# Conv2 in 21 matmuls a chunk instead of 24, with the work around it put in another order

## The chip, the cores and the metric

One core of a Trainium2 chip runs one launch that handles all 8 images. The metric is the time of that launch on the device in microseconds, lower is better. PE is the matmul engine, DVE, ACT and POOL are the vector, scalar and GpSimd engines, SP is the engine that here only issues DMAs. Each works through its own list of instructions, and semaphores tie the lists together.

## The reference, cut to what matters

x has shape 8 x 64 x 64 x 48. Four layers follow each other:

```python
# L0: linear attention over the 4096 pixels, then three convolutions, 96 channels inside
y = concatenate([attention(x), x])                # 96 channels
y = leaky_relu(conv1x1(y, w1) + b1, 0.2)          # conv1
y = leaky_relu(conv3x3(y, w2) + b2, 0.2)          # conv2, SAME padding, 96 -> 96
x1 = conv1x1(y, w3) + b3 + x                      # w3, 96 -> 48
# L1: relu, depthwise 3x3, pointwise 48 -> 48, batch norm
x2 = bn(pointwise(depthwise(relu(x1))))
# L2: experts mixed for each image
rw = sigmoid(mean(x2) @ Wr + br)                  # routing, 4 experts
h = relu(bn(x2 @ mix(Wpw, rw)))                   # expand, 48 -> 192
h = relu(bn(depthwise3x3(h, mix(Wdw, rw))))       # depthwise, 192 channels
x3 = bn(h @ mix(Wpwl, rw)) + x2                   # project, 192 -> 48
# L3: like L1
out = bn(pointwise(depthwise(relu(x3))))
```

## The kernel before

An image is cut into 8 chunks of 8 rows (512 pixels) at 96 channels, or 4 chunks of paired rows (`pair_conv`, m = 0 to 3) at 48 channels. Pairs means that two halves of the image lie beside each other on the partitions (even from row 0, odd from row 64).

The images are pipelined in three parts. In iteration f, PE runs conv2, w3, L1 and the first two expand chunks of image f; the attention and conv1 of image f+1 (`attn`); and the project, L3 and output of image f-1 (`back`), whose depthwise DVE computes beside conv2. The first iteration stands alone (no `back`), a hardware loop runs f = 1 to 6, and `last_iteration` finishes images 6 and 7 alone. The order on each engine is written out by hand in `iteration` of that engine; nothing else schedules.

What the steps below touch:

- **conv2** (L1247, L1252, L1258). The fp32 product is made of reduced-precision parts: high activations by low weights (9 taps, `w2_l` x `y1_h`, 96 rows), high activations and the last third of the low ones by high weights (9 taps, 128 rows, `w2_h` x part 0 of `y1_parts`), and the other two thirds of the low activations by high weights, packed over 128 rows (6 matmuls, `w2_two`, `w2_one`). `copy_thirds` on SP places the thirds after POOL (L1116) has computed the low part.
- **L1 and L3** (`l1`, `l3` = `pair_conv`, L1285 to L1288): 15 matmuls a chunk. Each chunk needs six DMAs (`copy_beside`, `beside_l1`, `beside_l3`) that place shifted copies beside the activations. They wait for the high and low parts of chunk m+1 as well (ACT, then DVE L789).
- **Depthwise** (L696): 48 steps of one tap over 1024 elements on DVE, and two first taps, in an order set by `tap_of_step`; how many stand beside each chunk of conv2 and between the later steps is the table `steps_at`. `project(back, (m,))` (L1334 to L1350) waits for the units that it reads, made nonnegative by ACT (`finish_unit`, L1549).
- **x2** is L1's output, high and low, in `y1_parts`. `copy_x2` moves it to `x_even` and `x_odd`, from which expand and project read, in 8 DMAs on SP (L1007).
- **Routing** (DVE L807, L809, PE L1294, DVE L814, ACT L1607): the mean over L1's output decides the mixed weights (`mix_weights`). The halo (`expand_halo`, first matmuls of L1300 and L1301) is the first to read them and x2.
- **Attention**: `transpose_x` (L1170), scores (L1181), squares on ACT, `norms_begin` on DVE (L619 to L621), `scale_k` on POOL (L1110), sums (L1193), gather, weights.

## Time and profile before

| | |
|---|---|
| Time, median of 3 runs | 1107.56 us (1106.48 to 1109.27) |
| The profiled execution, its own time | 1108.68 us, of which the span from first to last instruction is 1106.9 us |
| PE | 1030.5 us busy, 93% of the span |
| DVE | 872.8 us busy, 79% |
| ACT, POOL | 469.6 us and 92.6 us busy |
| Granted TensorE clock | 0.975 of full speed on average |
| DMA | one hardware queue, 86.84 MB |

Six iterations of the loop lie between 176.28 and 927.8 us of the span. The stretch ahead of them is the prologue and the first iteration, the one behind them the last. Lines such as L1285 are lines of the kernel before; a number in brackets at the end of a row is idle time just before it and what ended it.

### The profile page before, as it was taken

Reading aid. Unit: us, or ns where it says so; the run is one execution under the profiler, and the core shown is the slowest. Engines: PE = TensorE matmul, PEld = TensorE weight load, DVE = VectorE, ACT = ScalarE, POOL = GpSimd, SP = SyncE. Lnnn points to the kernel's source line nnn. Section 1 sums busy time; section 2 is a strip of 40 time slices with the busy share of each in tenths; the row PEclk is TensorE's granted clock in tenths of the full one; section 3 lists DMA queues with packets and bytes.
Section 4 is the critical chain, followed back from the end, with each engine's and each line's share of the span. In section 5 each row is a group of like instructions: output and inputs, shape, how many; then the busy total and the mean of one; then the engine's idle time right before and its main releaser. Section 6 shows DMA issues by size and latency. Waiting matters only on the chain.

```text
span 1106.9 us, 14973 instructions
## 1 busy us (share of the span) xinstructions
PE 1030.5 (93%) x4790; PEld 658.3 (59%) x4790; DVE 872.8 (79%) x1201; ACT 469.6 (42%) x813; POOL 92.6 (8%) x72
## 2 busy tenths in 40 slices
PE   4689969999999999999999999999999999999976
PEld 3456656666665676666665576666666576655524
DVE  6652579997699958998599958998599958998950
ACT  3311434345633645345632645255532645234431
POOL 0300012001300102001300103001300103000000
PEclk9799969999999999999999999999999999998998
DMA  5125416145432556145342456145442453146214
GB/s 70 41 57 76 99 30 102 26 98 122 91 51 50 107 125 101 24 97 114 85 62 49 103 127 105 24 89 110 96 64 49 103 116 74 22 86 137 40 26 101
DMA packets 124401, 87.19 MB, mean 79 GB/s; under 512 B 96880, under 2 KB 97749, under 8 KB 124373
## 3 DMA queue, kind: packets, MB, share of 16 engines
q1 hardware_dynamic: 124372, 86.84, 39.9%
q8 instruction: 15, 0.25, 0.1%
q14 instruction: 14, 0.11, 0.0%
HBM read 10.82 MB, written 6.29 MB: 15 GB/s over the span
## 4 chain that ended last, share of the span: by engine, by line
PE 70%; DVE 12%; issue 7%; SPq 4%; ACT 3%; DMA 3%; POOL 0%; ACTq 0%; DVEq 0%; POOLq 0%
PE bank L1247 13%; PE bank L1252 12%; PE bank L1258 8%; PE bank L1285 8%; PE bank L1228 5%; PE bank L1300 3%; PE bank L1269 3%; PE bank L1301 3%; DMA y_parts<-a_parts 2%; DVE s L619 2%; DVE a_parts L789 2%; PE bank L1350 2%; PE bank L1288 2%; DVE dwa L696 2%; PE bank L1287 2%
## 5 line engine op out<-in xcount | busy, mean ns | idle before, releaser
L696 DVE SCALAR_TENSOR_TENSOR dwa<-h1a,dyn,dwa 128x1024 f32<-128x1024 f32 x224 | 274.1, 1275 | 0.0
L1247 PE MATMUL bank<-y_parts,w_l 96*96 96x512 f32 x576 | 151.4, 408 | 0.0
L1252 PE MATMUL bank<-y_parts,w_h 128*96 128x512 f32 x576 | 147.3, 400 | 0.0
L696 DVE SCALAR_TENSOR_TENSOR dwb<-h1b,dyn,dwb 128x1024 f32<-128x1024 f32 x112 | 136.6, 1275 | 0.0
L1285 PE MATMUL bank<-a_parts,wt_h 128*112 128x512 f32 x384 | 118.1, 416 | 15.1 <-DMA y_parts<-a_parts 10.9
L1247 PEld LDWEIGHTS bank<-y_parts,w_l 96*96 96x96 f32 x576 | 91.6, 163 | 60.7 <-issue 21.3
L1252 PEld LDWEIGHTS bank<-y_parts,w_h 128*96 128x96 f32 x576 | 93.3, 162 | 44.2
L1285 PEld LDWEIGHTS bank<-a_parts,wt_h 128*112 128x112 f32 x384 | 64.0, 177 | 49.1 <-issue 23.1
L1116 POOL TENSOR_TENSOR y_parts<-y,y_parts 96x512 fp32r<-96x512 f32 x56 | 67.1, 1200 | 248.0 <-DVE y L750 248.0
L1561 ACT ACTIVATE y<-bank,b2s 96x512 f32<-96x512 f32 x32 | 21.9, 684 | 141.0 <-PE bank L1258 141.0
L1258 PE MATMUL bank<-y_parts,w_one 128*96 128x512 f32 x192 | 77.1, 401 | 0.0
L1258 PE MATMUL bank<-y_parts,w_two 128*96 128x512 f32 x192 | 76.7, 399 | 0.0
L1110 POOL TENSOR_TENSOR tok<-tok,u 128x1536 f32<-128x1536 f32 x8 | 24.6, 3073 | 586.3 <-DVE u L621 586.3
L1228 PE MATMUL bank<-xq,w_cur 97*96 97x512 f32 x128 | 68.1, 614 | 3.6 <-DVE y L750 3.6
L789 DVE SCALAR_TENSOR_TENSOR a_parts<-v,a_parts 112x512 fp32r<-112x512 f32 x64 | 59.0, 932 | 15.7 <-ACT a_parts L1590 12.9
L1561 ACT ACTIVATE xq<-bank,b2s 96x512 f32<-96x512 f32 x32 | 21.9, 685 | 116.0 <-PE bank L1258 107.4
L749 DVE TENSOR_TENSOR y_parts<-bank,y 96x512 fp32r<-96x512 f32 x64 | 43.9, 687 | 24.9 <-ACT y L1517 24.8
L1612 ACT ACTIVATE dwa<-bank,conv_bias,inv 112x512 f32<-112x512 f32 x28 | 21.8, 778 | 91.2 <-PE bank L1288 91.2
L1285 PE MATMUL bank<-a_parts,wt_l 128*112 128x512 f32 x192 | 56.6, 403 | 0.0
L1288 PE MATMUL bank<-y_parts,wt_h 128*112 128x512 f32 x128 | 51.3, 401 | 0.0
L1287 PE MATMUL bank<-y_parts,wt_h 128*112 128x512 f32 x128 | 51.1, 399 | 0.0
L1181 PE MATMUL bank<-qkw,xcm 113*128 113x192 f32 x256 | 49.4, 337 | 1.7 <-ACT xcm L1477 1.7
(263 smaller groups left out, 1714.3 us busy)
## 6 DMA issues: line engine op xcount, KB each, us to landing
y_parts<-a_parts SPq DMA_DIRECT2D x64, 198.0 KB, 3.0
y_parts<-a_parts SPq DMA_DIRECT2D x64, 197.6 KB, 3.4
tok<-in_x_dram SPq DMA_DIRECT2D x48, 192.0 KB, 4.9
a_parts<-a_parts SPq DMA_DIRECT2D x128, 66.0 KB, 2.4
y_parts<-y_parts SPq DMA_DIRECT2D x64, 131.9 KB, 2.3
x_even<-y_parts SPq DMA_DIRECT2D x32, 198.0 KB, 3.6
x_odd<-y_parts SPq DMA_DIRECT2D x32, 198.0 KB, 4.0
out_dram<-dwb SPq DMA_DIRECT2D x24, 192.0 KB, 3.6
```

The lines of the kernel that those rows point to most:

```text
L696: nc.vector.scalar_tensor_tensor(out=dst, in0=tap_input(n, t), scalar=weight, in1=dst, op0=ALU.mult, op1=ALU.add).then_inc(tap_step, 1)
L749: nc.vector.tensor_tensor(y1_view(y1_h, k - 1), bank.rearrange("p (j w) -> p j w", w=W), y1_tokens(k - 1), ALU.max).then_inc(y1h_ready, 1)
L789: return nc.vector.scalar_tensor_tensor(out=lo[:, rows, 1:W + 1], in0=src[:, m % 2, :].rearrange("p (j w) -> p j w", w=W), scalar=0.0, in1 ...
L1116: nc.gpsimd.tensor_tensor(y1_view(y1_l, k), y1_tokens(k), y1_view(y1_h, k).bitcast(F32), ALU.subtract).then_inc(y1l_ready, 1)
L1181: last = nc.tensor.matmul(bank[:, m * 2 * C2:(m + 1) * 2 * C2], xcm[:, i * 128:(i + 1) * 128], qkw[:, :], start=True, stop=True)
L1228: nc.tensor.matmul(bank[0:C2, :], w1_cur[:, :], xq[:, (k - 1) % 2, :], start=True, stop=True)\
L1247: nc.tensor.matmul(bank[0:C2, :], w2_l[:, t, :], y1_h[:, rows, cols], start=t == 0, stop=False)
L1252: nc.tensor.matmul(bank[0:C2, :], w2_h[:, t, :], y1_parts[:, 0, rows, cols], start=False, stop=False)
L1258: last = nc.tensor.matmul(bank[0:C2, :], wgt[:, kh, :], y1_parts[:, 1, rows, cols], start=False, stop=kh == 2 and kw == 2)
L1285: nc.tensor.matmul(bank[0:P2, :], wgt[layer][:, kw, :], own[:, rows, kw:kw + W], start=n + kw == 0, stop=False)
L1287: nc.tensor.matmul(bank[0:P2, :], wgt[layer][:, 3, :], beside[:, rows, 1:W + 1], start=False, stop=False)
L1288: last = nc.tensor.matmul(bank[0:P2, :], wgt[layer][:, 4, :], beside[:, rows, 2:W + 2], start=False, stop=n == 2)
```

## The change

- Conv2 takes 9 + 9 + 3 matmuls a chunk. `w2_l` grows to 128 rows (its last 32 hold high weights of the middle third), so that `y1_parts` part 0 carries the high activations and the low middle third. Part 1 is a copy of the high activations with the last low third. The first low third lies three times, shifted by 0, 1 and 2 columns, in `y1_low`, a tile of its own. This tile shares its memory with the attention's `tok`.
- So `copy_thirds` issues 5 DMAs a piece instead of 3 (one of 96 x 1056 values), POOL clears the edges of `y1_low` for each image, and `load_x` (next image's x into `tok`) waits for the end of conv2. It stands between `beside_l1` for quarters 0, 1 and for quarters 2, 3. DVE rewrites the column of ones in `tok` each iteration.
- The depthwise units run in the order of the projections: (0,2), (1,3), (4,5), with `steps_at` 6,3,3,4,3,4,3,3 beside conv2 and 3,1,4,13 behind it.
- PE: l1(1) stands ahead of project 0 and 1, all of `transpose_x` behind l1(2), l3(0) ahead of project 2 (in bank 1), all 32 sums ahead of the routing.
- `copy_x2` is 4 DMAs of twice the size, issued by ACT behind the routing's sigmoid instead of by SP in two halves. In the last iteration it stays on SP.
- The last iteration: l3(0) of image 6 ahead of the routing, l3(1) to l3(3) between expand chunks, the taps on PE in two parts, and units 3 and 4 of the last depthwise one behind the other instead of by turns.

```diff
-B_COPIES, WT_COPIES, X2_COPIES = 6, 24, 8
+B_COPIES, WT_COPIES, X2_COPIES = 6, 24, 4
...
+        with nc.sbuf_tensor("y1_low", [128, (H + 2) * WP], F32R) as y1_low:
+            y1_l = y1_low[0:C2, :].rearrange("p (h w) -> p h w", w=WP)
+        tok = sb("tok", [128, RUN, 2, TOK])
...
+        STEPS = in_turn(0, 2) + in_turn(1, 3) + in_turn(4, 5)
+        FINISHED = {0: 2, 1: 4, 2: 5, 3: 6}
-        steps_at = (0,) * CHUNKS + (7, 4, 4, 4, 4, 4, 4, 4) + (1, 1, 5, 8)
+        steps_at = (0,) * CHUNKS + (6, 3, 3, 4, 3, 4, 3, 3) + (3, 1, 4, 13)
...
-        LAST_STEPS = ([(n, t) for t in range(TAPS) for n in (0, 1)] + [(n, t) for t in range(1, TAPS) for n in (3, 4)]
-                      + [(5, t) for t in range(1, TAPS)])
+        LAST_STEPS = in_turn(0, 1) + in_turn(3) + in_turn(4) + in_turn(5)
...
             def iteration(f, attn, back):
                 conv2_out(f, back)
+                if attn is not None:
+                    nc.vector.memset(tok[:, :, :, ONE_AT], 1.0)
...
+                norms_begin(attn)
                 x2_low_part(f, 0)
+                if back is not None:
+                    l3_low_part(back, 2)
                 x2_low_part(f, 1)
-                norms_begin(attn)
                 x2_low_part(f, 2)
                 if back is not None:
-                    l3_low_part(back, 2)
+                    l3_low_part(back, 3)
                 mean_out(f)
                 x2_low_part(f, 3)
                 route(f)
-                if back is not None:
-                    l3_low_part(back, 3)
...
         def load_x(sp, image):
-            wait(sp, xqt_done, CHUNKS * image)
+            wait(sp, conv2_done, CHUNKS * image)
...
+                wait(sp, y1h_ready, CHUNKS * image + 2 * p + 2)
+                sp.dma_start(second[0:C2, :], first[0:C2, :]).then_inc(apart_copied[p], 16)
                 wait(sp, y1l_ready, POOL_CHUNKS * image + min(2 * p + 2, POOL_CHUNKS))
...
+                sp.dma_start(first[C2:128, :], low[THIRD:2 * THIRD, :]).then_inc(apart_copied[p], 16)
+                sp.dma_start(second[C2:128, :], low[2 * THIRD:C2, :]).then_inc(apart_copied[p], 16)
+                wait(sp, apart_copied[p], 48 * (image + 1))
+                for shift in (1, 2):
+                    sp.dma_start(low[shift * THIRD:(shift + 1) * THIRD, :-shift], low[0:THIRD, shift:]).then_inc(shifts_copied[p], 16)
...
                 route(f)
-                if attn is not None:
-                    fourth_powers(attn)
-                if back is not None:
-                    l3_out(back, (0,))
+                act.wait_ge(x2l_ready, PCHUNKS * f + PCHUNKS)
+                copy_x2(act)
+                fourth_powers(attn)
```

PE, conv2, one chunk in the loop. Before:

```order
L1247 MATMUL bank<-y_parts,w_l 96x512 x9
L1249 ISA
L1252 MATMUL bank<-y_parts,w_h 96x512 x9
L1254 REGISTER_ALU
L1258 MATMUL bank<-y_parts,w_two 96x512
L1258 MATMUL bank<-y_parts,w_one 96x512
L1258 MATMUL bank<-y_parts,w_two 96x512
L1258 MATMUL bank<-y_parts,w_one 96x512
L1258 MATMUL bank<-y_parts,w_two 96x512
L1258 MATMUL bank<-y_parts,w_one 96x512
```

The change:

```order
L1249 REGISTER_ALU
L1253 MATMUL bank<-y_parts,w_l 96x512 x9
L1253 MATMUL bank<-y_parts,w_h 96x512 x9
L1256 REGISTER_ALU
L1259 MATMUL bank<-y_low,w_row 96x512 x3
L87 REGISTER_ALU
```

The six single matmuls of `w_two` and `w_one` are gone; three of `w_row` stand in their place.

PE, from project 3 (`pick`, `pc`) to the first sums (`tok`) and the chunk of L3 (`wt_h`) that follows. Before, with the routing (`routed`) ahead of l3(0) and then the first half of the sums:

```order
L1334 MATMUL bank<-x_odd,pick 112x512
L1335 MATMUL bank<-x_even,pick 48x512
L1350 MATMUL bank<-dwa,pc 48x512 x2
L1350 MATMUL bank<-dwb,pc 48x512 x2
L1294 MATMUL bank<-wr,routed 128x4
...
L1285 MATMUL bank<-a_parts,wt_h 112x512 x3
L1287 MATMUL bank<-y_parts,wt_h 112x512
L1288 MATMUL bank<-y_parts,wt_h 112x512
...
L1193 MATMUL bank<-tok 48x97 x16
```

The change, where the chunk of L3 behind the routing is l3(1):

```order
L1331 MATMUL bank<-x_odd,pick 112x512
L1332 MATMUL bank<-x_even,pick 48x512
L1347 MATMUL bank<-dwa,pc 48x512 x2
L1347 MATMUL bank<-dwb,pc 48x512 x2
...
L1196 MATMUL bank<-tok 48x97 x32
L1290 MATMUL bank<-wr,routed 128x4
...
L1281 MATMUL bank<-a_parts,wt_h 112x512 x3
L1283 MATMUL bank<-y_parts,wt_h 112x512
L1284 MATMUL bank<-y_parts,wt_h 112x512
```

All 32 sums moved ahead of the routing, and l3(0) ahead of both projections; between the routing and l3(1) PE has nothing.

SP, between L3's first quarter and the next. Before, the first half of x2 is copied there:

```order
L945 REGISTER_ALU
L1007 DMA x_even<-y_parts 48x1056 x2
L1007 DMA x_odd<-y_parts 48x1056 x2
...
L972 DMA a_parts<-a_parts 16x2x528 x2
L972 DMA y_parts<-a_parts 16x2x528
L972 DMA y_parts<-a_parts 48x2x528
L976 DMA y_parts<-a_parts 16x2x527
L976 DMA y_parts<-a_parts 48x2x527
```

SP in the change, at the place where the loads of x stand, ahead of L1's quarter 2 (`a_parts`, then `y_parts`):

```order
L947 ISA
L960 ISA
L960 DMA tok<-in_x_dram 64x16x48
L960 ISA
L960 DMA tok<-in_x_dram 64x16x48 x3
L960 ISA
L960 DMA tok<-in_x_dram 64x16x48
L960 ISA
L960 DMA tok<-in_x_dram 64x16x48
L947 REGISTER_ALU x2
L974 DMA a_parts<-a_parts 16x2x528 x2
L974 DMA y_parts<-a_parts 16x2x528
```

The x2 copies left SP altogether, and the six loads of x moved from its start to this place, past two quarters of L1.

## Rows read from the trace of the kernel before

**Rows 1.** The page, section 1: busy microseconds, share of the span, instructions.

```profile
span 1106.9 us, 14973 instructions
...
PE 1030.5 (93%) x4790; PEld 658.3 (59%) x4790; DVE 872.8 (79%) x1201; ACT 469.6 (42%) x813; POOL 92.6 (8%) x72
```

**Rows 2.** Windows, one iteration of the loop: length, then busy time of each engine.

```profile
426.60:551.95 125.35, 122.34 (x589) 78.70 (x589) 106.85 (x137) 58.15 (x100) 11.51 (x8) 1.00 0.43 85
```

**Rows 3.** Windows, conv2 and the middle of one loop iteration.

```profile
426.60:475.99 49.39, 49.39 (x205) 31.59 (x206) 49.35 (x49) 13.95 (x17) 0.00 (x0) 1.00 0.34 53
475.99:515.90 39.91, 38.79 (x202) 23.82 (x200) 35.89 (x44) 25.55 (x50) 3.12 (x1) 1.00 0.49 102
```

**Rows 4.** Timeline of PE, the last part of one chunk of conv2 and the next.

```profile
436.60 0.40 PE L1258 MATMUL bank<-y_parts,w_two 128*96 128x512 f32 x1
...
438.02 2.30 PE L1247 MATMUL bank<-y_parts,w_l 96*96 96x512 f32 x9
```

**Rows 5.** Timeline of PE, from the end of project 2 to the halo.

```profile
502.45 1.03 PE L1350 MATMUL bank<-dwb,pc 128*48 128x512 f32 x4
...
510.21 0.35 PE L1294 MATMUL bank<-wr,routed 112*128 112x4 f32 x2 [0.66 <-DVE routed L809]
510.43 0.96 PE L1285 MATMUL bank<-a_parts,wt_h 128*112 128x512 f32 x3
...
514.16 1.54 PE L1193 MATMUL bank<-tok 128*48 128x97 f32 x32
516.69 0.94 PE L1285 MATMUL bank<-a_parts,wt_h 128*112 128x512 f32 x3 [0.98 <-DMA y_parts<-a_parts]
...
531.38 0.28 PE L1300 MATMUL bank<-x_even,ew_h 96*128 96x64 f32 x1
```

**Rows 6.** Timeline of DVE and POOL in the same stretch.

```profile
489.08 1.29 DVE L789 SCALAR_TENSOR_TENSOR a_parts<-v,a_parts 112x512 fp32r<-112x512 f32 x2
...
490.29 9.65 DVE L696 SCALAR_TENSOR_TENSOR dwa<-h1a,dyn,dwa 128x1024 f32<-128x1024 f32 x8
...
501.76 3.35 DVE L619 TENSOR_REDUCE s<-tok 128x64 f32<-128x3072 f32 x1 [0.61 <-ACT tok L1487]
...
506.01 3.12 POOL L1110 TENSOR_TENSOR tok<-tok,u 128x1536 f32<-128x1536 f32 x1 [79.50 <-DVE u L621]
...
506.39 3.29 DVE L789 SCALAR_TENSOR_TENSOR a_parts<-v,a_parts 112x512 fp32r<-112x512 f32 x1
```

**Rows 7.** Timeline of SP: DMA issues of x, L3's first copies, x2's second half.

```profile
431.36 5.79 SPq L958 DMA_DIRECT2D tok<-in_x_dram  x6
...
509.77 1.32 SPq L972 DMA_DIRECT2D a_parts<-a_parts  x2
...
522.96 1.22 SPq L1007 DMA_DIRECT2D x_even<-y_parts  x2
```

**Rows 8.** Timeline of DVE and PE, end of the first iteration.

```profile
133.49 3.35 DVE L619 TENSOR_REDUCE s<-tok 128x64 f32<-128x3072 f32 x1 [4.60 <-ACT tok L1487]
...
141.08 0.56 PE L1294 MATMUL bank<-wr,routed 112*128 112x4 f32 x2 [4.62 <-DVE routed L809]
...
141.57 5.01 PE L1193 MATMUL bank<-tok 128*48 128x97 f32 x64
...
153.74 0.42 PE L1300 MATMUL bank<-x_even,ew_h 96*128 96x64 f32 x1
```

**Rows 9.** Timeline of PE, end of the last iteration.

```profile
1040.33 23.36 PE L1328 MATMUL bank<-h1a,tok 128*128 128x512 f32 x54
...
1068.35 0.49 PE L1334 MATMUL bank<-x_odd,pick 96*112 96x512 f32 x1 [2.33 <-ACT dwa L1538]
...
1080.03 0.94 PE L1285 MATMUL bank<-a_parts,wt_h 128*112 128x512 f32 x3 [4.07 <-DMA y_parts<-a_parts]
```

**Rows 10.** Windows behind two idle times of PE: the third value from the end is the granted clock.

```profile
141.57:146.35 4.78, 4.78 (x65) 4.78 (x64) 3.95 (x15) 2.89 (x3) 0.00 (x0) 0.53 0.64 150
1068.35:1075.00 6.65, 6.65 (x28) 1.88 (x30) 3.52 (x6) 3.94 (x6) 0.00 (x0) 1.00 0.06 10
```

More of the change, by code:

```diff
@@ L186, in conv_chain_kernel @@
         y1_parts = sb("y1_parts", [128, 2, H + 2, WP], F32R)
-        y1_h, y1_l = (y1_parts[0:C2, part, :, :] for part in range(2))
+        y1_h, y1_h_again = (y1_parts[0:C2, part, :, :] for part in range(2))
         y2 = [t[0:C2, 0:2, :].rearrange("p a n -> p (a n)") for t in (xq, y1)]
@@ L318, in tap_input, with step_value @@
             return src[:, r0 + t // 3:r0 + t // 3 + UNIT_ROWS, t % 3:t % 3 + W]
[L320 to L333 removed]
+        def step_value(image, n, t):
+            return TAP_STEPS * image + STEPS.index((n, t)) + 1
         def last_unit(n):
@@ L982, in copy_thirds @@
                 rows = slice(1 + p * H // PIECES, 1 + (p + 1) * H // PIECES)
-                high, low = (y1_parts[:, part, rows, :].bitcast(F32).rearrange("p h w -> p (h w)") for part in range(2))
+                first, second = (y1_parts[:, part, rows, :].bitcast(F32).rearrange("p h w -> p (h w)") for part in range(2))
+                low = y1_l[:, rows, :].bitcast(F32).rearrange("p h w -> p (h w)")
+                wait(sp, y1h_ready, CHUNKS * image + 2 * p + 2)
+                sp.dma_start(second[0:C2, :], first[0:C2, :]).then_inc(apart_copied[p], 16)
                 wait(sp, y1l_ready, POOL_CHUNKS * image + min(2 * p + 2, POOL_CHUNKS))
@@ L1016, in store, with beside_l1 @@
                     sp.dma_start(dst[j, par][:, runs, :], src[:, par, runs, :]).then_inc(stored, 16)
-        def beside_l1(sp, f):
-            for m in range(PCHUNKS):
+        def beside_l1(sp, f, quarters):
+            for m in quarters:
                 chunks = min(m + 2, PCHUNKS)
@@ L1274, in pair_conv @@
                 for m in chunks:
-                    if layer == L3 and image is LAST - 1 and m == 0:
-                        pe.wait_ge(ah3_ready, PCHUNKS * image + 1)
-                        bank = ring.bank(places[m])
-                    else:
-                        bank = ring.take(pe, image, places[m])
+                    bank = ring.take(pe, image, places[m]) if places[m] is not None else first_l3
                     pe.wait_ge(b_copied[layer][m], 16 * B_COPIES * (image + 1))
@@ L1638, in iteration @@
                 l1_high_part(f, PCHUNKS - 1)
[L1639 to L1640 removed]
+                if back is not None:
+                    finish_unit(back, 1)
+                    finish_unit(back, 3)
                 l1_out(f, (0,))
```

298 lines of the change are left out of this document (138 added, 160 removed).

## The prediction

> **What bounds the kernel now.** I first read the page's busy times: PE works 1030.5 of 1106.9 us [rows 1]. Such a share says that matmuls taken away should show, unless something else stands close behind. Then the windows: an iteration of the loop takes 125.35 us with PE busy for 122.34 and DVE for 106.85, and the clock is full [rows 2]. By stage, DVE is as busy as PE beside conv2 (49.35 of 49.39 us) and has 35.89 of the next 39.91 [rows 3]. So the loop has two limits. PE sets the pace of conv2, but from its end on a second chain runs nearly abreast: depthwise on DVE, project on PE, the low part on DVE, six DMAs, then L3. Its places are in the timelines: the last eight depthwise steps begin at 490.29 and take 9.65 [rows 6], project 2 ends at about 503.4, the first copies behind it are issued at 509.77 [rows 7], and the chunk of L3 that needs them starts at 516.69, having waited 0.98 for a DMA [rows 5]. The question is how much of what PE saves reaches the halo, which starts at 531.38 [rows 5]; conv1 and expand behind it are not touched.
>
> **Conv2's matmuls.** Six of them take 438.02 - 436.60 = 1.42 us [rows 4], 0.237 each. Three fewer in 8 chunks are 5.7 us an image, 45.6 us over 8 images. The whole of conv2 would end at 470.3 instead of 475.99 in this iteration. POOL's six small memsets and SP's two more DMAs a piece lie in the 20 us of conv1, where I cost them at nothing: conv2 of the next image reads the pieces one by one, and the cover is the 6 us that one chunk of conv2 lasts (an eighth of 49.39, rows 3). If it is gone, they cost up to 1 us an image.
>
> **From conv2 to L3 in the loop.** A chunk of L1 or L3 takes 3.73 us in the trace (510.43 to the sums at 514.16 [rows 5]); inside a dense stretch I take 3.65. Project takes 2.4 a chunk, w3 and each 8 transposes 1.0, four groups of scores 3.0, half of the sums 1.5 (1.54 for the 32 matmuls, rows 5). From 470.3: l1(0), w3, l1(1) and two projections end at 483.4. Next is l1(2). Its copies now stand on SP behind the six loads of x, and these wait for the end of conv2. They take 5.79 us to issue [rows 7], so until about 477.9. From a quarter's first issue to its matmul it is 516.69 - 509.77 = 6.92 us [rows 5, 7]. So l1(2) can start at 484.8, a **new wait of 1.4 us** (up to 1.9, since the loads of x still move when the copies start). Before, x was loaded at 431.36 [rows 7], beside conv2, and delayed nobody. Then come l1(2), all transposes with 0.5 us until ACT has handed the last over, the scores with l1(3) between, and 0.7 for the squares: 501.5. L3's chunk 0 goes to 505.2 and project 2 to 507.6. That is **4.2 us later than project 2 ends now**, although conv2 is 5.7 shorter, because l3(0), l1(3) and half of the scores are ahead of it. DVE's depthwise ends at about 501 instead of 499.94 [rows 6]: its steps are the same work and it has waits of 2 to 3 us for PE and ACT. It would bound project 2 only if PE were some 4 us faster.
>
> **What DVE and POOL do there.** Norms come ahead of the low parts now. The low part of L3 at 506.39 took 3.29 us [rows 6] where two others take 1.29 together (at 489.08, rows 6), and POOL's scaling runs over the same time (3.12 from 506.01 [rows 6]). In the change this clash meets the low part of x2 instead (norms 501.1 to 505.2), and L3's low part of chunk 2, which waits for project 2 anyway, is ready at 507.6 + 1.3 (ACT) + 0.7 = 509.6. So the clash leaves the chain, and this gives back what the later project 2 costs: SP issues at 509.6, now it does at 509.77. L3's chunk 1 starts at 516.5, now 516.69. The Trainium skill, "SBUF — State Buffer", on the shared port pair, says that a DVE operation with two SBUF inputs and a GpSimd operation that reads SBUF hold this pair as an exclusive lock and the loser blocks; these two rows agree.
>
> **The gap.** PE has project 3 until 510.0, sums until 513.0, routing at 513.2, then nothing before 516.5: **an idle time of 3.3 us**, where before l3(0) and sums stood. What PE saved in conv2 lies idle here and in the waits above (3.3 + 1.4 + 0.5 + 0.7 = 5.9). Behind it the quarters' copies follow at SP's pace of some 4.4 us (six issues of about 0.66, two in 1.32 in rows 7, and waits), so l3(2) starts at about 521.0 and l3(3) at 525.4, and the halo at 525.4 + 3.7 + weights and output tokens 1.3 = 530.4. Now it is 531.38. The gain is **1.0 us an iteration**, from 0.7 to 1.2 by the rounding of these steps, 6 us in six.
>
> **x2 on ACT's queue.** SP loses eight DMAs of about 0.6 us of issuing, the last four from 522.96 [rows 7]; none is on the chain, since L3's copies go first. On ACT the four stand behind the sigmoid, about 515.5 to 518, and hold back the fourth powers by 2.6 us, which gather then has to absorb. They move 1.6 MB beside L3's quarters 2 and 3. In the trace all goes over one queue, so it shows no two side by side. Bounds: nothing (the bytes fit into the gaps between quarters), or all of their time, which is 4 x 198 KB in the 3.25 us of issuing and landing twice over, 7 us. I take nothing for the likeliest case and come back to the rest below.
>
> **The first iteration loses.** It has no projections and no L3 as cover. The copies for l1(2) wait behind the x loads (about 5.4 us of PE idle, against 5.7 saved in conv2), and the last scores come later: squares end at 137, now at 133.49 [rows 8]. Norms, POOL's scaling and now all sums are ahead of the routing. Routing is at 141.08 [rows 8]. In the change the sums start at 144.3 (137.1 + 4.1 + 3.1) and take 2.95 at full or 5.01 as they do now [rows 8] at the lower clock, so routing is at 147.4 to 149.8. The 12.7 us from it to the halo (153.74, rows 8) are DVE's and ACT's and stay. Cost: +6.3 to +8.7, taken as **+7.5**.
>
> **The last iteration gains.** Conv2 gives 5.7, and the chunks of L3 lie between expand chunks instead of between expand and the taps, which start at 1040.33 [rows 9]; in the change at 1031 to 1036, by whether the clock holds. Against that, the units 3 and 4 one behind the other make each step wait for the one before, +1.8 us. Both projections are split around the taps, so the wait of 2.33 at 1068.35 shrinks, the wait of 4.07 at 1080.03 [rows 9] hardly. I take **-8**, from -6 to -11. The prologue gets +0.5 for a larger weight table.
>
> **Sum.** -6 + 7.5 - 8 + 0.5 = -6 us. The profiled execution took 1108.68 us, 1.1 over the median, and 1.8 more than its span. I put the difference on the median: 1107.56 - 6 = **1101.5 us**. A measurement tells about 0.3% from no change, 3.3 us, so faster means under 1104.2.
>
> **Rivals.**
> 1. *The end keeps the clock, the chain holds* (above): 1101.5, range 1093 to 1109. Chance 0.32.
> 2. *More reaches the halo.* My steps put project 2 at 507.6 by adding hand-offs one after the other. If l1(2)'s copies are early and the gap at l3(1) is half as long, an iteration gains 3 to 5 us: 6 x -4 instead of -6, so 1083, and 1073 to 1093 by the ends. For it: PE has only 116.6 us of work left in 124 us, and DVE 107. Against: the copies' 6.9 us are a fixed latency. Chance 0.22.
> 3. *PE alone is the bound and all 45.6 us show*: 1062. Against it stands DVE beside conv2, 49.35 of 49.39 [rows 3], and the chain. Chance 0.04.
> 4. *Slower, by the clock.* PE idles 3.3 us at 513.2 in each iteration. In the first iteration, behind 4.62 us of idle time [rows 8], the granted clock is 0.53 in the next 4.78 us [rows 10], and the 64 sums take 5.01 instead of the 2.9 that they take at full speed. After 2.33 us of idle time at 1068.35 [rows 9] it stayed at 1.00 [rows 10]. 3.3 lies between. Of TensorE's two levels, 1.2 and 2.4 GHz, the lower makes a chunk of L3 last 7.3 instead of 3.65. If that holds for 3.4 us, the loss is 1.7 us; if it holds for l3(1) and l3(2), 7.3. It decides from 1 us a time on, where it eats the gain. With 3.5 us a time: 6 x (3.5 - 1) + 0 = +15 against -6 of the loop, so 1101.5 + 21 = 1122; with 1.7, 1112. The Trainium skill, "TensorE: Matmul & The Clock Gate", has the clock return to the lower level when PE idles, which speaks against a rewoven order that leaves such a gap; the rows agree for the long gap and not for the short one. Chance 0.24.
> 5. *x2 in the way of L3.* If the two queues are served by turns, the long rows of x2 (8448 bytes) against 2112 of the quarters' take most of the time from 517 to 524. L3's chunk 2 would come 4 us late, at 525, and the halo at 534 instead of 530.4: +2.6 us against now, 6 x 3.6 = 22 over my forecast, 1123; if shared by bytes, +1 to 1.5 us, about 1109. The Trainium skill, "DMA: Bandwidth & Descriptors", says under "Queues, rings and completion order" that each DMA engine goes round between queues a packet at a time, and under "Issuing engines are not separate DMA queues" that another issuing engine saves only sequencer time. By this rule the second queue brings no bandwidth. No run here shows it. Chance 0.18.
>
> **How the numbers follow.** Case 1 is faster in 0.23, same in 0.08, slower in 0.01; case 2 and 3 faster in 0.26; case 4 and 5 split 0.02, 0.08 and 0.32. Together faster 0.51, same 0.16, slower 0.33. For 8 in 10 the range goes from case 2's lower end, 1073, to 1126, past the middle of cases 4 and 5: it leaves out case 3, an edge of case 2, and what lies over 3.5 us an iteration. Case 1 alone has 1093 to 1109.
>
> **What would show it.** Conv2's windows must be 43.7 us; if they are longer, PE waits in it for `y1_low`. l1(2) waits for a DMA (1.4 us) at some 57 us into the iteration. Project 2 ends 81 us into it, and PE idles some 3.3 us ahead of l3(1) for a DMA. Granted clock: 1.00 through the loop, or 0.5 behind that gap (case 4). The time from l3(1) to l3(2) is 4.4 us, or 8 (case 5). The first iteration is 6 to 9 us longer from conv2's end to the halo. The prediction is wrong if the iteration takes under 123 or over 126 us.

## The result, and the profile after

The changed kernel takes 1189.64 us (median of 4 runs, 1187.74 to 1192.26) against 1108.21 us of the kernel before: a ratio of 1.074, 95% interval 1.0717 to 1.0762. It is **81 us slower**. The page of the changed kernel, sections 1 and 3:

```profile
span 1185.9 us, 14639 instructions
...
PE 1013.9 (85%) x4598; PEld 649.4 (55%) x4598; DVE 862.6 (73%) x1207; ACT 472.9 (40%) x813; POOL 96.1 (8%) x120
...
q1 hardware_dynamic: 125652, 92.78, 38.7%
q10 hardware_dynamic: 1792, 11.36, 4.8%
```

PE has 16.6 us less busy time than in [rows 1], not 45.6, because part of its work now runs at the lower clock, and the span is 79 us longer. There is a second hardware queue, q10: ScalarE's, with x2. The two queues move 104.1 MB, against 86.84 MB before: conv2's new copies are 17 MB more.

The first matmul of conv2 in each image cuts the span into pieces (in the kernel before at 60.38, 176.12, ... 927.64 us, in the changed one at 58.97, 188.85, ... 1016.07). Loop is the mean of six iterations. The first four columns are read from the profiled execution, the last is the median of all runs. The two can differ: the profiled execution of `before_late_x` was 4.6 us faster than its median and that of `late_x_21` 6.3 us, while that of `x2_act_timed` was 5.2 us slower. The table has all kernels that the next section tells of:

| kernel | ahead of conv2 of image 0 | first iteration | loop, one iteration | last | time, median us |
|---|---|---|---|---|---|
| before | 60.4 | 115.7 | 125.25 | 179.2 | 1108.2 |
| changed | 59.0 | 129.9 | 137.87 | 169.8 | 1189.6 |
| before_x2_act | 60.9 | 118.8 | 136.25 | 181.2 | 1181.3 |
| x2_sp_early | 60.7 | 117.4 | 137.65 | 181.0 | 1184.7 |
| x2_act_timed | 60.8 | 120.7 | 128.56 | 181.2 | 1130.7 |
| x2_on_sp | 61.4 | 128.1 | 132.97 | 171.4 | 1156.7 |
| x2_halves | 61.5 | 126.3 | 130.40 | 169.6 | 1139.7 |
| halves_fillers | 58.4 | 126.8 | 126.77 | 170.5 | 1119.6 |
| before_21 | 58.6 | 110.0 | 124.70 | 178.8 | 1095.4 |
| before_late_x | 58.3 | 118.6 | 125.64 | 174.8 | 1112.1 |
| late_x_21 | 61.2 | 114.4 | 125.27 | 173.3 | 1108.5 |
| fillers | 61.2 | 129.1 | 135.78 | 185.0 | 1188.3 |
| l3_0_behind | 61.3 | 128.0 | 132.90 | 170.0 | 1158.1 |
| load_x_last | 61.2 | 134.7 | 138.61 | 171.4 | 1200.4 |
| before_fillers | 60.7 | 115.3 | 125.31 | 174.2 | 1103.9 |
| late_x_21_fillers | 61.3 | 109.8 | 125.79 | 172.6 | 1100.6 |

Of the 79.0 us of span, 6 x 12.6 = 75.7 are lost in the loop and 14.1 in the first iteration; the last gives back 9.4 and the prologue 1.4. The prologue says nothing of the change: it takes 58.3 to 61.5 us in these kernels, whatever they change.

One iteration of the loop by stage (length, busy time of PE, PEld, DVE, ACT, POOL, granted clock, DMA share, GB/s): conv2, its end to l3(1), l3(1) to the halo, and the rest.

```profile
603.14:646.71 43.57, 43.57 (x181) 27.69 (x181) 42.86 (x44) 13.95 (x17) 0.17 (x3) 1.00 0.28 66
646.71:697.47 50.76, 41.96 (x234) 26.69 (x233) 39.07 (x46) 24.59 (x49) 3.11 (x1) 0.97 0.55 96
697.47:721.12 23.65, 16.95 (x64) 12.21 (x64) 8.70 (x24) 5.85 (x8) 0.00 (x0) 0.78 0.54 111
721.12:741.57 20.45, 19.70 (x92) 12.41 (x90) 14.29 (x26) 14.20 (x27) 8.67 (x12) 1.00 0.49 118
```

Conv2 takes 43.57 us, 5.8 less than in [rows 3], and the last stage 20.45, as before (20.57). The two in the middle took 40.70 us (475.99 to 516.69 in [rows 5]) and 14.69 (to the halo); now they take 50.76 and 23.65. The granted clock is below 1.00 in both.

PE in these stages (start, length; in brackets the idle time just before and what ended it):

```profile
652.69 0.96 PE L1281 MATMUL bank<-a_parts,wt_h 128*112 128x512 f32 x3 [1.26 <-DVE v L776]
...
663.97 1.59 PE L1281 MATMUL bank<-a_parts,wt_h 128*112 128x512 f32 x3 [2.61 <-DMA y_parts<-a_parts]
...
682.00 0.96 PE L1281 MATMUL bank<-a_parts,wt_h 128*112 128x512 f32 x3 [0.72 <-ACT tok L1479]
...
693.50 0.36 PE L1290 MATMUL bank<-wr,routed 112*128 112x4 f32 x2
697.47 1.12 PE L1281 MATMUL bank<-a_parts,wt_h 128*112 128x512 f32 x3 [3.62 <-DMA y_parts<-a_parts]
...
709.49 1.59 PE L1281 MATMUL bank<-a_parts,wt_h 128*112 128x512 f32 x3 [6.34 <-DMA y_parts<-a_parts]
...
716.65 0.97 PE L1281 MATMUL bank<-a_parts,wt_h 128*112 128x512 f32 x3 [0.35 <-ACT dwa L1605]
...
721.12 0.28 PE L1296 MATMUL bank<-x_even,ew_h 96*128 96x64 f32 x1
```

Three idle times end with a DMA: 2.61 us ahead of l1(2), 3.62 ahead of l3(1), 6.34 ahead of l3(2). Before, there was one of 0.98 [rows 5]. SP's queue there, where a length is the time that issuing took:

```profile
649.25 5.84 SPq L960 DMA_DIRECT2D tok<-in_x_dram  x6
655.50 1.53 SPq L974 DMA_DIRECT2D a_parts<-a_parts  x2
...
690.41 1.25 SPq L974 DMA_DIRECT2D a_parts<-a_parts  x2
...
694.72 3.38 SPq L974 DMA_DIRECT2D a_parts<-a_parts  x2
698.14 4.92 SPq L974 DMA_DIRECT2D y_parts<-a_parts  x2
703.11 3.72 SPq L978 DMA_DIRECT2D y_parts<-a_parts  x2
```

The six loads of x go out at 649.25, ahead of L1's quarter 2. L3's quarter 1 takes 3.9 us to issue from 690.41. Its quarter 2 takes 12.1 us from 694.72, three times as long. ACT's queue at that time:

```profile
694.34 1.73 ACTq L1006 DMA_DIRECT2D x_even<-y_parts  x2
...
696.10 5.22 ACTq L1006 DMA_DIRECT2D x_odd<-y_parts  x2
```

x2's four copies are issued from 694.34 to 701.3, the last two at 2.6 us each. Clock in the windows from l3(1) to l3(2), and over most of l3(2):

```profile
697.00:709.49 12.49, 5.68 (x20) 4.07 (x20) 8.81 (x23) 4.08 (x5) 0.00 (x0) 0.81 0.85 171
709.49:715.40 5.91, 5.91 (x15) 4.25 (x16) 0.00 (x0) 0.00 (x0) 0.00 (x0) 0.53 0.42 93
```

Each of the three idle times has a stretch at the lower level behind it (0.53 of full speed in the second window, so near 1.2 GHz of the two levels), in which a chunk of L3 lasts 6.1 us instead of 3.65.

The end of the first iteration, which answers to [rows 8]:

```profile
120.39 1.59 PE L1281 MATMUL bank<-a_parts,wt_h 128*112 128x512 f32 x3 [5.66 <-DMA y_parts<-a_parts]
...
146.26 5.42 PE L1196 MATMUL bank<-tok 128*48 128x97 f32 x64 [8.19 <-POOL tok L1105]
...
152.36 1.24 ACTq L1006 DMA_DIRECT2D x_even<-y_parts  x2
153.63 4.92 ACTq L1006 DMA_DIRECT2D x_odd<-y_parts  x2
158.59 1.51 ACT L1483 ACTIVATE dwa<-tok 128x1536 f32<-128x1536 f32 x1 [6.04 <-issue]
...
163.06 0.56 PE L1204 MATMUL bank<-twin,routed 112*97 112x48 f32 x2 [10.94 <-DVE routed L644]
```

The ACT row at 158.59 is the fourth powers, which can't start before ACT has issued x2's four copies (152.36 to 158.55).

### The profile page after: what moved, and what is told of

Read it like the earlier page. It is cut to its first block, busy times and chain, and to the rows that moved or that the text cites. A ratio compares the mean times of both kernels' runs of the same rounds, so it can differ in the third digit from the quotient of the medians.

```text
span 1185.9 us, 14639 instructions
## 1 busy us (share of the span) xinstructions
PE 1013.9 (85%) x4598; PEld 649.4 (55%) x4598; DVE 862.6 (73%) x1207; ACT 472.9 (40%) x813; POOL 96.1 (8%) x120
## 4 chain that ended last, share of the span: by engine, by line
PE 59%; SPq 14%; DVE 10%; DMA 5%; ACT 5%; issue 5%; ACTq 1%; POOL 0%; DVEq 0%; POOLq 0%
PE bank L1253 22%; PE bank L1281 9%; SPq L974 8%; DMA y_parts<-a_parts 5%; PE bank L1233 4%; PE bank L1259 4%; PE bank L1184 4%; SPq L978 3%; SPq L960 3%; PE bank L1284 3%; PE bank L1283 3%; PE bank L1296 2%; PE bank L1347 2%; DVE dwa L709 2%; PE bank L1297 2%
## 5 line engine op out<-in xcount | busy, mean ns | idle before, releaser
L1281 PE MATMUL bank<-a_parts,wt_h 128*112 128x512 f32 x384 | 129.8, 450 | 98.5 <-DMA y_parts<-a_parts 79.2
L1253 PE MATMUL bank<-y_parts,w_l 128*96 128x512 f32 x576 | 151.1, 407 | 0.0
L1281 PEld LDWEIGHTS bank<-a_parts,wt_h 128*112 128x112 f32 x384 | 71.5, 198 | 139.1 <-issue 77.2
L1253 PEld LDWEIGHTS bank<-y_parts,w_l 128*96 128x96 f32 x576 | 91.5, 163 | 60.6 <-issue 21.2
L1112 POOL TENSOR_TENSOR y_low<-y,y_parts 96x512 fp32r<-96x512 f32 x56 | 67.2, 1200 | 307.8 <-DVE y L747 307.8
L786 DVE SCALAR_TENSOR_TENSOR a_parts<-v,a_parts 112x512 fp32r<-112x512 f32 x64 | 44.1, 689 | 49.3 <-ACT a_parts L1582 46.5
L1281 PE MATMUL bank<-a_parts,wt_l 128*112 128x512 f32 x192 | 66.1, 459 | 0.0
L1259 PE MATMUL bank<-y_low,w_row 96*96 96x512 f32 x192 | 56.3, 402 | 0.0
L1284 PE MATMUL bank<-y_parts,wt_h 128*112 128x512 f32 x128 | 55.0, 430 | 0.0
L1283 PE MATMUL bank<-y_parts,wt_h 128*112 128x512 f32 x128 | 54.9, 429 | 0.0
L615 DVE TENSOR_REDUCE s<-tok 128x64 f32<-128x3072 f32 x8 | 26.8, 3353 | 34.6 <-ACT tok L1479 34.6
```

The costliest lines, as they stand in the source:

```text
L786: return nc.vector.scalar_tensor_tensor(out=lo[:, rows, 1:W + 1], in0=src[:, m % 2, :].rearrange("p (j w) -> p j w", w=W), scalar=0.0, in1 ...
L1112: nc.gpsimd.tensor_tensor(y1_view(y1_l, k), y1_tokens(k), y1_view(y1_h, k).bitcast(F32), ALU.subtract).then_inc(y1l_ready, 1)
L1253: nc.tensor.matmul(bank[0:C2, :], wgt[:, t, :], y1_parts[:, part, rows, cols], start=part + t == 0, stop=False)
L1259: last = nc.tensor.matmul(bank[0:C2, :], w2_row[:, kh, :], y1_l[:, rows, cols], start=False, stop=kh == 2)
L1281: nc.tensor.matmul(bank[0:P2, :], wgt[layer][:, kw, :], own[:, rows, kw:kw + W], start=n + kw == 0, stop=False)
L1283: nc.tensor.matmul(bank[0:P2, :], wgt[layer][:, 3, :], beside[:, rows, 1:W + 1], start=False, stop=False)
```

## Experiments

Times are medians, in brackets the 95% interval of the ratio to the kernel before, which was measured again beside each group of runs. Sums over the loop are six iterations of the table.

**Where x2's copies stand.** Five kernels are about this. `x2_on_sp` is the changed kernel with the copies moved:

```diff
-                act.wait_ge(x2l_ready, PCHUNKS * f + PCHUNKS)
-                copy_x2(act)
                 fourth_powers(attn)
...
                     beside_l3(sp, back, f + 1)
+                wait(sp, x2h_ready, PCHUNKS * f + PCHUNKS)
+                wait(sp, x2l_ready, PCHUNKS * f + PCHUNKS)
+                copy_x2(sp)
```

> The changed kernel with one part undone: in the first seven iterations SP issues the four copies of x2 behind L3's last quarter, not ScalarE behind the routing. Theory A (the copies on the second queue hold up SP's issues for L3's quarter 2): the quarter's six issues take 4 us again instead of 12, the wait of 6.3 us ahead of l3(2) shrinks to about 1, the clock stays up there, and an iteration takes 129 to 131 us instead of 138.4: 1135 to 1150 us in all. Theory B (the gap and the lower clock behind it cost the time, wherever x2 is issued): the chunk of L3 behind it stays late, an iteration takes 136 or more, 1175 to 1190 us.

1156.69 us [1.0393, 1.0482], 33 us less than the changed kernel. l3(2) no longer waits for a DMA; of x2, what is left is the halo, which waits 2.03 us for it now. Theory A, but its number (1135 to 1150) did not come, and neither did its clock: the idle times of 2.36 us ahead of l1(2) and 3.50 ahead of l3(1) are still there, and the granted clock is 0.96 over the loop.

`before_x2_act` does the reverse: the kernel before, with SP's copies of x2 taken out and these lines of the change put in. (In the last iteration they stay on SP, as in the change, all four together ahead of L3's quarter 1.)

```diff
-B_COPIES, WT_COPIES, X2_COPIES = 6, 24, 8
+B_COPIES, WT_COPIES, X2_COPIES = 6, 24, 4
...
                 route(f)
+                act.wait_ge(x2l_ready, PCHUNKS * f + PCHUNKS)
+                copy_x2(act)
```

> The kernel before with only this part of the change: x2 in four large copies on ScalarE's queue behind the routing (in the last iteration on SP). Theory A: L3's quarters 2 and 3 come late here too, an iteration takes 5 to 8 us more, 1140 to 1155 us. Theory B (it is the new order around it that hurts): 1105 to 1115 us.

1181.32 us [1.0655, 1.0703]: this one edit costs 73 us, 11.0 an iteration, far over theory A's 5 to 8 and nearly as much as the whole change lost. PE of this kernel at L3's chunk 1, and SP's issues for it:

```profile
687.14 1.59 PE L1278 MATMUL bank<-a_parts,wt_h 128*112 128x512 f32 x3 [9.90 <-DMA y_parts<-a_parts]
```

```profile
672.60 3.40 SPq L972 DMA_DIRECT2D y_parts<-a_parts  x2
676.04 6.28 SPq L976 DMA_DIRECT2D y_parts<-a_parts  x2
```

The last two of its six copies take 6.28 us to issue, where such a pair takes 1.34, and the chunk waits 9.90 us.

Is it the second queue or the moment? `x2_act_timed` is the kernel before with its eight small copies on ACT, issued at about SP's moments:

```diff
                     finish_unit(back, 5)
+                act.wait_ge(x2l_ready, PCHUNKS * f + 2)
+                issue_x2(act, 0)
                 l1_out(f, (2,))
...
                     root_of_q(attn)
+                act.wait_ge(x2l_ready, PCHUNKS * f + PCHUNKS)
+                issue_x2(act, 1)
```

> The kernel before with x2's eight copies of 198 KB on ScalarE's queue at about the times at which SP issues them before: the first four behind the last unit's finish, the other four behind the root of q. Theory A1 (it is the moment that hurts: all of x2 beside L3's quarter 1): 1105 to 1115 us, since the moments are those of before. Theory A2 (a second queue holds up SP's issues by itself): L3's copies are late here too, 1125 us or more.

`x2_sp_early` is `before_x2_act` with the four copies on SP, between L3's quarters 0 and 1:

```diff
                     beside_l3(sp, back, f + 1, (0,))
+                wait(sp, x2h_ready, PCHUNKS * f + PCHUNKS)
+                wait(sp, x2l_ready, PCHUNKS * f + PCHUNKS)
+                wait(sp, project_done, 2 * PCHUNKS * f)
+                copy_x2(sp)
```

> The kernel before with x2 in four large copies on SP's queue, all between L3's quarters 0 and 1, so ahead of quarter 1 on one queue, at the moment of ScalarE's issue in the change. Theory A1 (moment and volume): l3(1) comes as late as with ScalarE's queue, 7 to 9 us an iteration, 1150 to 1185 us, close to the 1181 of the run with ScalarE. Theory A2 (the second queue is what hurts): clearly faster than that run, under 1145 us.

`x2_sp_early` takes 1184.68 us [1.0641, 1.0726], the same as with ACT's queue, which is theory A1. Its l3(1) waits even longer, on one queue:

```profile
554.10 1.59 PE L1282 MATMUL bank<-a_parts,wt_h 128*112 128x512 f32 x3 [11.37 <-DMA y_parts<-a_parts]
```

Here SP issues the quarter's copies only from 544.42, behind x2's, where on ACT's queue they were issued at once but slowly.

`x2_act_timed` takes 1130.7 us [1.0132, 1.0238], in runs that spread from 1124.6 to 1135.9: 3.3 us an iteration over the kernel before. By its number that is theory A2, but the trace shows a collision again. l3(1) starts 90.5 us into the iteration, before it was 90.2, and SP issues its copies at the old pace. It is the second half of x2 that is not quite at its old moment: before, SP issued it behind quarter 3's copies; now ACT issues it (535.72 to 539.87) while SP is still at them (533.04 to 537.81), and l3(3) waits for a DMA, with the lower clock behind it:

```profile
535.67 2.14 SPq L976 DMA_DIRECT2D y_parts<-a_parts  x2
```

```profile
535.72 0.52 ACTq L1011 DMA_DIRECT2D x_even<-y_parts  x1
```

```profile
543.30 0.94 PE L1287 MATMUL bank<-a_parts,wt_h 128*112 128x512 f32 x3 [2.03 <-DMA y_parts<-a_parts]
...
544.55 1.29 PE L1287 MATMUL bank<-a_parts,wt_l 128*112 128x512 f32 x3
```

So the moment is what hurts: 1.6 MB at once ahead of or beside L3's quarters, on either queue. Two things these runs don't separate. Wherever all of x2 goes at one moment, it also goes as four large copies instead of eight. And whether a second queue at exactly the old moments would cost anything was not run.

`x2_halves` undoes the x2 part of the change as a whole: eight copies on SP at the places of the kernel before, and the DVE order for them:

```diff
                     beside_l3(sp, back, f + 1, (0,))
+                copy_x2(sp, f, 0)
+                if back is not None:
+                    beside_l3(sp, back, f + 1, range(1, PCHUNKS))
+                copy_x2(sp, f, 1)
...
+                x2_low_part(f, 0)
+                x2_low_part(f, 1)
                 norms_begin(attn)
-                x2_low_part(f, 0)
                 if back is not None:
                     l3_low_part(back, 2)
-                x2_low_part(f, 1)
```

> The changed kernel with the whole x2 part undone: eight copies of 198 KB on SP, the first four between L3's quarters 0 and 1, the other four behind quarter 3, and the first two low parts of x2 ahead of the norms on DVE. Theory A1 (all of x2 at one moment near the halo is what hurts): the halo no longer waits for x2, some 2 to 3 us an iteration less than with the four copies behind L3's quarters (1156.7 us), 1135 to 1148 us. If it stays at 1152 or above, x2's volume was not what the halo waited for.

1139.67 us [1.0247, 1.0322], within theory A1's range; the halo no longer waits. The x2 part as a whole costs 50 us in the changed kernel.

**The clock.** `fillers` puts matmuls of constants into the changed kernel's three idle times:

```diff
+                    for _ in range({(L1, 2): 8, (L3, 1): 14, (L3, 2): 24}.get((layer, m), 0)):
+                        nc.tensor.matmul(bank[0:P2, :], wt_h[layer][:, 0, :], w2_h[:, :, :].rearrange("p t o -> p (t o)")[:, 0:BANK],
+                                         start=True, stop=True)
                     pe.wait_ge(b_copied[layer][m], 16 * B_COPIES * (image + 1))
```

> The changed kernel with matmuls of constants (into the bank that the next chunk overwrites) in the three idle times: 8 ahead of l1(2), 14 ahead of l3(1), 24 ahead of l3(2), 1.9, 3.3 and 5.7 us at full clock. Theory C (the lower clock behind the idle times is a cost of its own): the granted clock is 1.00 in the loop, PE's work shrinks by some 5 us an iteration, 1150 to 1165 us. Theory A alone (PE only waits for the copies): the time stays within 1180 to 1195 us, since the waits end when the copies land.

1188.25 us [1.0698, 1.0756], which is in the range of theory A alone. But an iteration of the loop takes 135.78 instead of 137.87, at a clock of 0.99 instead of 0.94. The total hides it, since the last iteration, where nothing waits there, pays for its fillers (185.0 us instead of 169.8). So the clock's share was only 2.1 us an iteration while x2 held everything up. `halves_fillers` asks again without x2 in the way, in the loop alone:

```diff
+                    for _ in range({(L1, 2): 9, (L3, 1): 13}.get((layer, m), 0) if not isinstance(image, int) else 0):
```

> The same kernel, with matmuls of constants in the two idle times of the loop that are left: 9 ahead of l1(2), 13 ahead of l3(1), 2.1 and 3.1 us at full clock. Theory C (the lower clock behind the idle times costs 1.4 us or more behind each): the clock stays at 1.00 in the loop and an iteration takes 1.5 to 3 us less, so 9 to 18 us in all. If the chain over DVE and the copies decides alone: no difference, or some slower where a filler overruns.

1119.59 us [1.0091, 1.0154], **20 us less**. One iteration of each, `x2_halves` first:

```profile
580.78:710.64 129.86, 119.70 (x565) 77.08 (x565) 104.90 (x138) 58.72 (x100) 11.64 (x16) 0.97 0.49 98
```

```profile
565.51:692.26 126.75, 122.09 (x587) 78.57 (x587) 104.90 (x138) 58.72 (x100) 11.64 (x15) 1.00 0.49 101
```

PE executes more (122.09 us busy with 5.6 us of fillers, against 119.70) and the iteration is 3.1 us shorter in these windows, 3.6 in the mean of six. Theory C, and a little over its 9 to 18 us. l3(1) starts 92.5 us into the iteration here. So with x2 undone and the clock at its upper level, the new order still reaches l3(1) 2.3 us later than the old one (90.2), although conv2 is 5.8 shorter.

**The chain into L3.** `l3_0_behind` is `x2_on_sp` with two steps of PE changed round:

```diff
-                    pe.wait_ge(squared, 16 * attn + 16)
-                    l3(back, (0,))
                     project(back, (2, 3))
+                    pe.wait_ge(squared, 16 * attn + 16)
+                    l3(back, (0,))
```

> The changed kernel with x2 on SP behind L3's quarters (1156.7 us) and l3(0) behind projections 2 and 3 instead of ahead of them. Theory D (l3(0) ahead of project 2 delays the chain into L3's copies): project 2 ends about 2 us earlier, so does l3(1), 2 us an iteration, 1143 to 1150 us. Theory E (that chain is set by DVE's norms and ScalarE, not by PE): within 3 us of 1157.

1158.13 us [1.041, 1.0498], no difference to 1156.69. Project 2 does start earlier. Then two others take over, on DVE and at the halo:

```profile
670.75 2.91 DVE L786 SCALAR_TENSOR_TENSOR a_parts<-v,a_parts 112x512 fp32r<-112x512 f32 x1 [0.29 <-ACT a_parts L1586]
```

```profile
666.71 0.50 PE L1335 MATMUL bank<-x_odd,pick 96*112 96x512 f32 x1 [1.59 <-ACT dwa L1545]
...
697.94 0.30 PE L1300 MATMUL bank<-x_even,ew_h 96*128 96x64 f32 x1 [3.19 <-DMA x_odd<-y_parts]
```

L3's low part now meets POOL's scaling and takes 2.91 us, and the halo waits 3.19 us for x2. Theory E holds in its number; the reason is three chains nearly abreast.

**The late load of x.** `load_x_last` is `x2_on_sp` with `beside_l1(sp, f, range(PCHUNKS))` ahead of `load_x`:

> The changed kernel with x2 on SP behind L3's quarters, and the loads of x behind all of L1's quarters instead of between 1 and 2. Theory F (the late loads of x are in the way wherever they stand, since y1_low holds their memory until conv2 ends): l1(2) starts 1 to 2 us earlier, but the transposes behind it wait for x; an iteration takes 2 to 4 us more, 1165 to 1185 us. Theory G (only their place ahead of quarter 2 hurts): the wait of 2.4 us goes, 1140 to 1148 us.

1200.43 us [1.0789, 1.087], 44 us more than `x2_on_sp`: theory F, and beyond its number. PE at the transposes:

```profile
682.45 3.74 PE L1176 MATMUL bank<-ident,tok 128*112 128x128 f32 x16 [8.84 <-DMA tok<-in_x_dram]
```

`before_late_x` makes the load late in the kernel before:

```diff
             wait(sp, xqt_done, CHUNKS * image)
+            wait(sp, conv2_done, CHUNKS * image)
...
-                if attn is not None:
-                    load_x(sp, attn)
-                beside_l1(sp, f)
+                beside_l1(sp, f, (0, 1))
+                if attn is not None:
+                    load_x(sp, attn)
+                beside_l1(sp, f, (2, 3))
...
-                    transpose_x(attn, (2, 3))
+                    transpose_x(attn, range(4))
```

> The kernel before with x loaded late: the load waits for the end of conv2 and stands between L1's quarters 1 and 2 on SP, and the first half of the transposes moves to the second, behind l1(1). All 24 matmuls, x2 and the rest as before. Theory F (the late load costs by itself, about 2 us ahead of l1(2) or the transposes and the clock behind it): 3 to 5 us an iteration, 1125 to 1140 us. Theory H (there is room for it in the order before): within 5 us of 1108.

1112.06 us [1.0023, 1.0063]: theory H, at a cost of some 3 to 4 us in all. There l1(2) stands behind all transposes and four groups of scores, and waits for nothing.

**Conv2 alone.** `before_21` leaves three of the six packed matmuls out (`for wgt, kw in ((w2_two, 0),)`), nothing else.

> The kernel before with three of the six packed matmuls of each conv2 chunk left out, so a part of the low activations' product is missing; all else, order and copies, as before. It takes 45.6 us of matmuls from PE and adds nothing. If the chain over DVE, project and L3's copies is what ends last: 1095 to 1107 us. If PE is the bound: 1062 to 1070 us.

1095.43 us [0.9853, 0.9915], 12 us of 45.6, at the edge of the first theory's range. In the table 5.8 of them come in the first iteration, 0.55 in each of the loop, 0.4 in the last; 1.8 are the prologue's spread. But in the loop it is not the chain into L3 that takes the rest. PE waits for DVE's part of conv2's output, three times an iteration: 0.16, 0.89 and

```profile
592.21 1.97 PE L1269 MATMUL bank<-y,w3p 96*64 96x512 f32 x4 [2.24 <-DVE y L768]
```

These are 3.3 of the 5.7 us. The last one is followed by the lower clock (1.97 us for four matmuls that take 1.08 otherwise); the granted clock is 0.96 from 588 to 631 us, where it was 1.00 before, and that accounts for most of what is left. l3(1) starts 89.6 us into the iteration, 0.5 earlier than before. In the changed kernel, with 29 depthwise steps beside conv2 instead of 35, PE waits for nothing there. That the shorter table does it is an inference: the old order with only that table changed was not run. `late_x_21` has the real thing: `before_late_x` with all of the change's conv2, its copies, `y1_low` and its edges.

> The kernel before with the whole conv2 part of the change (21 matmuls, y1_low in the memory of tok, five copies a piece, edges on POOL, the load of x behind the end of conv2 and between L1's quarters 1 and 2), its transposes behind l1(1), and everything else in the order before. Theory I (the order around conv2 made the change slow, not conv2): about the sum of the runs with 3 matmuls left out (-12 us) and with the late load (+3 to +4), 1096 to 1102 us. Theory J (the copies and the shared memory eat the saving): 1106 us or more.

1108.52 us [0.9979, 1.002]: no slower and no faster than before, and by the two ratios some 0.4% faster than `before_late_x`, which has the same late load. The number is theory J's; some 8 us that the two runs with one half each had promised are gone, and which of the copies, the edges or the memory takes them was not told apart. PE waits where w3 stands here too, for DVE's part of conv2's output (up to 2.26 us), but `before_21` has the same waits, so they don't explain these 8 us:

```profile
226.51 1.08 PE L1280 MATMUL bank<-y,w3p 96*64 96x512 f32 x4 [2.26 <-DVE y L770]
```

**A version that beats both.** The kernel before has stretches at the lower clock in its first and last iteration. This is where the one in the last begins:

```profile
1011.00:1013.40 2.40, 1.29 (x4) 0.68 (x4) 2.31 (x9) 0.19 (x1) 0.00 (x0) 0.92 0.29 46
1013.40:1015.00 1.60, 1.51 (x4) 1.22 (x5) 0.69 (x2) 0.00 (x0) 0.00 (x0) 0.50 0.73 144
```

`before_fillers` puts constants ahead of them:

```diff
+                    fill(banks[6], 19)
                 routing(f)
...
+                    fill(banks[6], 15)
                 attention_gather(attn)
...
+                    fill(banks[6], 9)
                 attention_weights(attn)
...
+                    if n == 1:
+                        fill(banks[0], 5)
                     expand(f, n)
...
-                project(f, range(PCHUNKS))
+                project(f, (0,))
+                fill(banks[5], 9)
+                project(f, (1, 2, 3))
+                fill(banks[5], 16)
```

> The kernel before, with matmuls of constants in idle times of PE that lie ahead of stretches at the lower clock: 19, 15 and 9 in the first iteration ahead of the routing, the gather and the weights; 5, 9 and 16 in the last ahead of expand chunk 1, projection 1 and the first L3 chunk. Theory C: the clock stays at its upper level in 153.7 to 160, 1013.4 to 1027 and 1081.6 to 1085, which saves 3, 3 and 1.7 us on the path, 1099 to 1103 us, faster than both kernels. If the idle times alone set these stretches: within 3 us of 1108.

1103.86 us [0.9927, 0.9971], theory C in its kind and at the weak end of its 1099 to 1103. The clock is at its upper level from 1008 to 1026, where it was at half from 1013.4 to 1027:

```profile
1008.00:1026.00 18.00, 16.82 (x66) 9.69 (x62) 16.74 (x28) 11.25 (x23) 0.00 (x0) 1.00 0.54 113
```

The last iteration takes 174.2 us instead of 179.2, the first hardly less.

That stretch is no fixed part of the old order, though. `before_late_x` has the same last iteration and nearly the same idle times there (1.21, then 0.28 us; 1.21 and 0.22 in the kernel before), and in its profiled execution the clock stays at 1.00 and the last iteration takes 174.8 us. The kernel before itself took 1103.27 us in the one of 14 runs where the mean granted clock was 0.982, and 1113.09 in one where it was 0.971. The nine runs of `before_fillers` lie between 1100.76 and 1105.76.

`late_x_21_fillers` has the same fillers on `late_x_21`:

> The same kernel with the matmuls of constants in the idle times of the first and the last iteration, as in the run before_fillers (4 us faster than before). If the clock's share there is independent of conv2: 3 to 5 us less than late_x_21, 1092 to 1098 us. If the shorter conv2 leaves these idle times longer than the fillers cover: within 2 us of late_x_21.

**1100.59 us [0.9893, 0.9944]**, 0.8% faster than before and the lowest median here of a kernel that leaves nothing out. It is 7.9 us less than `late_x_21`, more than either theory said. Its interval overlaps that of `before_fillers` [0.9927, 0.9971], so it is not shown that conv2 in 21 matmuls adds anything to the fillers.

## Why the prediction was wrong

The forecast was 1101.5 us, range 1073 to 1126; the result is 64 us above the range, and the mechanism failed, not only the size. The steps, by the iteration of the rows above against the working from 470.3 on:

1. **Conv2's matmuls.** 5.7 us an image were forecast, 5.8 came (49.39 to 43.57), and the copies and memsets added no wait in conv2. Right. That the saving would hardly reach the halo came true as well, but in `before_21`, which keeps 0.55 us an iteration of it, DVE beside conv2 and the clock take it, not the chain into L3.
2. **From conv2 to l3(1).** 46.2 us were forecast (470.3 to 516.5), 50.76 came. The step that l1(2) starts 14.5 us behind conv2 failed: it is 17.3. The loads of x are issued until 655.09, 8.4 us behind conv2's end and not 7.6. The copies then take 8.5 us from first issue to matmul (655.50 to 663.97), not the 6.92 that the text called a fixed latency; the loads of x, still moving when they start, are the likely cause, which no run isolates. And the clock behind that wait takes another 1.5. (l1(1) waits 1.26 us for w3's output on DVE, which the working did not have; it costs nothing, since l1(2) waits for its copies anyway.) The rest of the walk to project 2 held within half a microsecond.
3. **"I take nothing for the likeliest case"** for x2 is the step that decided. The gap was forecast at 3.3 and is 3.62; but l3(2) came 12.0 us behind l3(1), not 4.4. The 7.6 us more are about all of x2's transfer (the upper bound of the text, 7 us): the DMA engines are busy for 0.85 of these 12 us, SP's issues slow down, and with the copies on SP behind L3's quarters the wait ahead of l3(2) is gone. Rival 5 had this mechanism with 4 us late and 2.6 over before; here it is 7.6, and in `before_x2_act` 11.0 an iteration with the clock behind it. The second queue changes nothing, as the pair 1181.3 and 1184.7 us shows. The Trainium skill says in "DMA: Bandwidth & Descriptors", under "Issuing engines are not separate DMA queues", that copies issued by different engines run on the same DMA engines, and that another issuing engine saves only issuing time. The pair agrees. The text had this as a rival with a chance of 0.18, and nothing of it in the sum.
4. **The clock.** Rival 4 was right as well, and both came at once. The text went by the length of the last idle time: 0.5 behind 4.62 and 3.77 us, none behind 2.33. Its own trace has the lower level from 1013.4 to 1027 as well (0.51 on average), where no idle time just ahead is over 1.21 us; that was overlooked. In the changed kernel the clock fell behind 2.61, 3.62 and 6.34. It costs 3.6 us an iteration where `halves_fillers` shows it by itself (3.3 by the medians), the 3.5 that the rival was priced at. The text added the rivals as alternatives, 21 and 22 us over the forecast, but nothing makes them exclusive: without x2's delay the idle times of 2.46 and 3.54 us in `x2_halves` lower the clock all the same, and x2's delay adds a third.
5. **l3(2) to the halo**: forecast 9.4 us, 11.6 came (709.49 to 721.12), since l3(2) ran at the lower clock.
6. **The first iteration** was forecast at +7.5 and lost 14.1. Routing starts 92.6 us behind the start of conv2, where it was 80.7: 11.9 later, not 6.3 to 8.7. From there to the halo it is 14.9 us, which the text kept at 12.7. These 2.2 are x2's: ACT is held for 6.2 us by issuing the four copies, not 2.6, so the fourth powers, DVE's copy of the sums behind them and the gather at 163.06 come late. In `x2_halves` that stretch takes 12.5. Why routing comes so late was not tested. **The last** was forecast at -8 and gained 9.4. The number is right, partly by luck: it is read against an execution of the kernel before in which the clock was at its lower level from 1013.4 to 1027. Against the 174.8 us of `before_late_x`, where it was not, the gain is 5.0.

Together: of 81 us, x2 is 50 (1189.6 to 1139.7), and the clock behind the two other idle times 20 (to 1119.6). The rest of 11 is, by the table, 11.1 in the first iteration and 9.1 in the loop, less what the last and the prologue give back; in the loop it is the later l3(1), whose cause is argued in step 2 and not tested by itself. Conv2 in 21 matmuls as a package, with its copies and the late load, is neither faster nor slower in the order before.

## What to carry to other kernels

Price a transfer that is moved by all its bytes at the rate that the trace shows, placed ahead of what shares the DMA engines with it, whichever engine issues it. Mechanisms that can come together belong in one case of a forecast, not in several: here a late copy left PE idle, and behind that idle time the clock fell. And before an order is rewoven to make room for fewer matmuls, leave the matmuls out in the old order: here that shows 12 us of 46, and its trace shows what takes the rest, DVE beside conv2 and then the clock.
